# Cross-attention and feed-forward kernel: residual stream kept with features on partitions

## The reference

```python
x   # (8, 128, 512); ctx (8, 128, 512); 32 heads of 128
n = layernorm(x)                     # no weights
h = rmsnorm(n) * ln_weight
q, k, v = h @ w_q.T, ctx @ w_k.T, ctx @ w_v.T          # (8, 128, 32 x 128)
s = where(mask, q k^T + position_bias, -inf)           # per batch and head
x = x + n + (softmax(s), masked) v @ w_out.T           # x + (n + attention)
n = layernorm(x)
W = NF4_CODE[w_codes] * absmax (blocks of 64)          # 512 x 512
x = x + n @ W.T + 2.0 * n @ W_a @ W_b
return x
```

## Time and profile before

| what | value |
|---|---|
| median of 3 runs | 832.5 us (832.13 to 833.02) |
| profiled execution, its own time | 831.71 us |
| span from first to last instruction | 829.9 us |
| busy: PE, DVE, ACT, Pool | 824.1, 447.5, 445.6, 535.3 us |
| instructions | 15761 |
| DMA | 64.46 MB, 78 GB/s on the mean |

### The profile page before, as it was taken

How to read it: one execution, slowest core, us unless ns; L and a number is a source line. 1 busy time by engine, 2 the same in 40 slices (tenths; PEclk the granted TensorE clock), 3 DMA queues, 4 the chain that set the end, 5 groups by cost and what they waited for, 6 DMA issues and landing times.

```text
span 829.9 us, 15761 instructions
## 1 busy us (share of the span) xinstructions
PE 824.1 (99%) x4702; PEld 720.3 (87%) x4702; DVE 447.5 (54%) x754; ACT 445.6 (54%) x1297; POOL 535.3 (65%) x556
## 2 busy tenths in 40 slices
PE   9999999999999999999999999999999999999998
PEld 6888888988899888988889888998889888898886
DVE  5785655355634656245553556346562455636683
ACT  5766474464726555364644647355553646447632
POOL 0576778467875778756785578757787567855440
PEclk9999999999999999999999999999999999999999
DMA  8212332122211323113221222113230232311102
GB/s 326 90 42 90 107 94 68 54 92 66 93 36 58 98 68 97 26 69 98 79 89 54 92 66 92 38 55 97 69 96 24 71 98 68 104 41 51 46 13 89
DMA packets 50357, 64.46 MB, mean 78 GB/s; under 512 B 10752, under 2 KB 36480, under 8 KB 49312
## 3 DMA queue, kind: packets, MB, share of 16 engines
q1 hardware_dynamic: 50336, 64.20, 24.9%
HBM read 44.24 MB, written 4.19 MB: 58 GB/s over the span
## 4 chain that ended last, share of the span: by engine, by line
PE 94%; DVE 2%; ACT 2%; SPq 1%; DMA 0%; issue 0%; POOL 0%; POOLq 0%; ACTq 0%
PE w_ps L1184 44%; PE o_ps L1184 35%; PE s_ps L1220 6%; PE s_ps L1226 6%; SPq L342 1%; ACT p_blocks L652 1%; DVE stats L901 1%; DVE resid L1017 1%; PE s_ps L1184 1%; ACT p_blocks L603 1%; PE s_ps L1250 0%; PE o_ps L1250 0%; PE w_ps L1286 0%; PE w_ps L1241 0%; PE w_ps L1247 0%; DMA pT<-p_blocks 0%
## 5 line engine op out<-in xcount | busy, mean ns | idle before, releaser
L531 POOL TENSOR_SCALAR picked<-codes 128x256 f32<-128x256 int32 x112 | 124.3, 1110 | 19.2 <-POOL level L534 15.6
L496 POOL TENSOR_TENSOR p<-pos_raw,mask_add 128x1024 f32<-128x1024 f32 x32 | 69.6, 2175 | 103.1 <-ACT p_blocks L652 102.8
L652 ACT ACTIVATE p_blocks<-p,neg_max 128x128 f32<-128x128 f32 x248 | 96.1, 389 | 48.4 <-DVE neg_max L994 44.0
L534 POOL TENSOR_TENSOR level<-level,picked 128x256 f32<-128x256 f32 x112 | 90.6, 809 | 20.9 <-POOL picked L531 20.9
L468 POOL TENSOR_TENSOR ring_lo<-k_raw,ring_hi 128x256 fp32r<-128x256 f32 x105 | 76.5, 740 | 30.2 <-ACT ring_hi L603 27.3
L603 ACT ACTIVATE ring_hi<-k_raw 128x256 fp32r<-128x256 f32 x105 | 38.8, 414 | 101.0 <-POOL k_raw L458 101.0
L1017 DVE TENSOR_TENSOR resid<-o_ps,resid 128x512 f32<-128x512 f32 x102 | 68.7, 686 | 44.7 <-PE o_ps L1184 44.5
L1184 PE MATMUL w_ps<-ctx_hi,ring_hi 128*128 128x512 f32 x210 | 84.7, 403 | 0.0
L1184 PE MATMUL w_ps<-ctx_hi,ring_lo 128*128 128x512 f32 x210 | 82.1, 391 | 0.0
L1184 PE MATMUL w_ps<-ctx_lo,ring_hi 128*128 128x512 f32 x210 | 81.7, 389 | 0.0
L603 ACT ACTIVATE p_blocks<-p_blocks,row_scale 128x128 f32<-128x128 f32 x248 | 77.2, 391 | 1.1 <-DVE row_scale L1001 1.1
(11 more groups left out here) (229 smaller groups left out, 2289.8 us busy)
## 6 DMA issues: line engine op xcount, KB each, us to landing
pT<-p_blocks SPq DMA_DIRECT2D x480, 32.0 KB, 1.8
k_raw<-k_dram SPq DMA_DIRECT2D x16, 512.0 KB, 3.5
wv_raw<-wv_dram SPq DMA_DIRECT2D x8, 1024.0 KB, 4.8
q_raw<-q_dram SPq DMA_DIRECT2D x32, 256.0 KB, 3.7
wo_raw<-wo_dram SPq DMA_DIRECT2D x32, 256.0 KB, 4.0
resid<-x_dram SPq DMA_DIRECT2D x2, 1024.0 KB, 12.6
pos_raw<-pos_dram SPq DMA_DIRECT2D x32, 64.0 KB, 3.8
out_dram<-resid SPq DMA_DIRECT2D x8, 256.0 KB, 2.0
```

The lines of the kernel that those rows point to most:

```text
L496: pool.tensor_tensor(p[:, :, :], pos, mask_add[:, :, :], ALU.add).then_inc(bias_done, 1)
L531: then(pool.tensor_scalar((level if code == 0 else picked)[:, :], codes[:, :], float(code), NF4[code], match, ALU.mult))
L534: then(pool.tensor_tensor(level[:, :], level[:, :], picked[:, :], ALU.add))
L652: e = act.activation(out(b), p[:, b, :].rearrange("p (k c) -> p k c", c=Q), ACT.Exp, bias=neg_max[:, b:b + 1], accum_out=prob_sum[:, b:b + 1])
```

## The change

The residual stream is kept with features on partitions: `resid` is [128 features, 4 slices, 1024 tokens].

- Start: x is loaded as before to the same memory for statistics and staging, and then a second copy of x, transposed on the host (`xt_d`), is loaded over it. It is multiplied by 1 + rstd, which is now a value per column: the 1024 scales go through DRAM and come back as a row on all partitions (`scale_row`, in `wo_raw`). The shift by the mean is left out of the stream. `residual(c)`: four operations of 128x1024. The loads of the first output weights wait for them.
- Loop: `output(t)` has w_out stationary and the attention moving; t runs over four slices of features for the first half of the tokens and then for the second.
- Feed-forward weights: centred, that is, the mean over input features is subtracted from each column, so that the stream needs no centring before the product. Pool sums the slices (two adds in the last group ahead of the last decode, one after the last slice has come), TensorE multiplies the sum by a 128x128 matrix of 1/512 between the attends of the two halves, DVE subtracts it (`centre_ffn`) between the adds of the last pair, ACT makes the high and Pool the low parts. The splitting in the last group goes.
- Tail: the stream itself is split (`stream_high`, `stream_low`) and multiplied. The stream is turned back to tokens on partitions for the output (`turn_back`), ACT adds the shift of the first norm (`shift`, into `v`), DVE takes the statistics from that, Pool rstd, and one DVE operation makes product * rstd + v. `ffn_norm`, `ffn_transpose` and `xT_low` go.

The diff, cut to its core (declarations left out):

```diff
@@ -171,7 +174,12 @@
 ...
         x_stage = [wv_raw[:, i, :] for i in range(4)] + two_tiles(flat_blocks(pT[:, :, :, :])) + [v[:, b, :] for b in (4, 5)]
-        ffn_stage = [kT[:, i, f * D:(f + 1) * D] for i in range(2) for f in range(2)]
+        x_tokens = flat(resid[:, :, :]).rearrange("p (b d) -> p b d", b=B)
+
+        scale_row = flat(wo_raw[:, :, :])
+
+        ffn_sum = flat(k_raw[:, 0:2, :])
+        mean_of = absmax[:, 0:P]
@@ -368,15 +382,27 @@
 ...
+            sp.wait_ge(factors_done, 1)
+            sp.dma_start(scale_d.rearrange("(b l) -> l b", b=B), ln_scale[:, :],
+                         allow_slow_non_contiguous=True).then_inc(scale_moved, 16)
+
+            sp.wait_ge(staged, B)
+            for i in range(2):
+                sp.dma_start(resid[:, 2 * i:2 * i + 2, :], xt_d[:, 2 * i:2 * i + 2, :]).then_inc(xt_loaded[i], 16)
+
+            sp.wait_ge(scale_moved, 16)
             sp.wait_ge(ctx_lo_done, 5)
-            load_wo(0, 0)
-            load_wo(1, 1)
+            sp.dma_start(scale_row, scale_d.partition_broadcast(P)).then_inc(scale_moved, 16)
 ...
+
+            sp.wait_ge(hidden_done, C)
+            load_wo(0, 0)
+            load_wo(1, 1)
@@ -548,6 +574,13 @@
 ...
                             split_k(m, p_at, key_slot(j, p_at))
+                    if last and j == 2:
+
+                        passed(ffn_loaded, 16)
+                        passed(k_lo_done, PRODUCTS * PAIRS)
+                        pool.tensor_tensor(ffn_sum, wv_raw[:, 0, :], wv_raw[:, 1, :], ALU.add).then_inc(ffn_sums, 1)
+                        passed(ffn_sums, 1)
+                        pool.tensor_tensor(ffn_sum, ffn_sum, wv_raw[:, 2, :], ALU.add).then_inc(ffn_sums, 1)
@@ -589,13 +622,18 @@
 ...
+            pool.memset(mean_of, 1.0 / D).then_inc(mean_of_done, 1)
+            pool.wait_ge(last_ffn_loaded, 16)
+            pool.wait_ge(ffn_sums, 2)
+            pool.tensor_tensor(ffn_sum, ffn_sum, wv_raw[:, C - 1, :], ALU.add).then_inc(ffn_sums, 1)
+            for c in range(C):
+                pool.wait_ge(ffn_hi_done, c + 1)
+                lo(ffn_weights(ctx_lo, c), wv_raw[:, c, :], ffn_weights(ctx_hi, c)).then_inc(ffn_lo_done, 1)
 ...
                 norm(pool.tensor_scalar(rms_a[:, one], mean_var[:, b, 1:2], EPS, None, ALU.add))
-                norm(pool.tensor_tensor(rstd[:, one], rms_a[:, one], minus_half[:, one], ALU.pow))
-                pool.tensor_scalar(ln_shift[:, one], mean_var[:, b, 0:1], rstd[:, one], -1.0,
-                                   ALU.mult, ALU.mult).then_inc(norm_done, 1)
+                pool.tensor_tensor(rstd[:, one], rms_a[:, one], minus_half[:, one], ALU.pow).then_inc(norm_done, 1)
@@ -678,6 +716,7 @@
 ...
             def split_ffn(c):
+                act.wait_ge(ffn_centred, c + 1)
@@ -798,12 +837,6 @@
 ...
                     split_wo(i, 2 * g + j // 2 + 1, wo_hi)
-                if last:
-
-                    act.wait_ge(ffn_loaded, 16)
-                    act.wait_ge(keys_done, PRODUCTS * m + 2)
-                    for c in range(C - 1):
-                        split_ffn(c)
@@ -868,26 +901,33 @@
 ...
-            act.wait_ge(last_ffn_loaded, 16)
-            split_ffn(C - 1)
-
-            def ffn_norm(b):
-                act.wait_ge(norm_done, 2 + b + 1)
-                if b >= 4:
-                    act.wait_ge(ffn_turned, b - 4 + 1)
-                act.activation(ffn_stage[b % 4], resid[:, b, :], ACT.Identity, bias=ln_shift[:, b:b + 1],
-                               scale=rstd[:, b:b + 1]).then_inc(ffn_staged, 1)
-
-            ffn_norm(0)
-            ffn_norm(1)
-            for b in range(B):
-                if b in range(2, B - 1):
-                    ffn_norm(b + 1)
-                act.wait_ge(ffn_turned, b + 1)
-                copy(xn_hi[:, :, b * L:(b + 1) * L],
-                     w_ps[b % 2][:, :].rearrange("p (c t) -> p c t", c=C)).then_inc(xT_hi_done, 1)
-                if b == 1:
-                    ffn_norm(2)
+
+            act.wait_ge(keys_done, PRODUCTS * PAIRS)
+            for c in range(C):
+                split_ffn(c)
+
+            def stream_high(b):
+
+                act.wait_ge(out_added, B * (PAIRS - 1) + HB * (b // HB + 1))
+                at = slice(b * L, (b + 1) * L)
+                copy(xn_hi[:, :, at], resid[:, :, at]).then_inc(xT_hi_done, 1)
+
+            def shift(b):
+
+                act.wait_ge(returned, b + 1)
+                act.activation(v[:, b, :], w_ps[b % 2][:, :], ACT.Identity, bias=ln_shift[:, b:b + 1]).then_inc(shifted, 1)
+
+            act.wait_ge(queries_done, 2 * H)
+            act.wait_ge(attn_done, 2 * H)
+            stream_high(0)
+            shift(0)
+            for b in range(1, HB + 1):
+                stream_high(b)
+            for b in range(1, B):
+                shift(b)
+                if b + HB < B:
+                    stream_high(b + HB)
@@ -933,16 +965,17 @@
 ...
                 dve.wait_ge(power_done, 3)
-                x_norm(dve.tensor_scalar(ln_scale[:, :], rstd[:, :], 1.0, None, ALU.add), False)
-                x_norm(dve.scalar_tensor_tensor(ln_shift[:, :], mean_var[:, :, 0], -1.0, rstd[:, :],
-                                                ALU.mult, ALU.mult))
-
-            def residual(b):
-
-                dve.wait_ge(staged, b + 1)
-                dve.tensor_scalar(resid[:, b, :], resid[:, b, :], ln_scale[:, b:b + 1], ln_shift[:, b:b + 1],
-                                  ALU.mult, ALU.add).then_inc(hidden_done, 1)
+                dve.tensor_scalar(ln_scale[:, :], rstd[:, :], 1.0, None, ALU.add).then_inc(factors_done, 1)
+                dve.scalar_tensor_tensor(ln_shift[:, :], mean_var[:, :, 0], -1.0, rstd[:, :],
+                                         ALU.mult, ALU.mult).then_inc(factors_done, 1)
+
+            def residual(c):
+
+                dve.wait_ge(xt_loaded[c // 2], 16)
+                dve.wait_ge(scale_moved, 32)
+                dve.tensor_tensor(resid[:, c, :], resid[:, c, :], scale_row, ALU.mult).then_inc(hidden_done, 1)
@@ -1013,23 +1046,22 @@
 ...
-            def add(b, bank):
-                dve.tensor_tensor(resid[:, b, :], bank, resid[:, b, :], ALU.add).then_inc(out_added, 1)
-
-            def add_pair(o, b):
-
-                dve.wait_ge(out_done, B * o + b + 1)
-                if b == 0:
-                    dve.wait_ge(hidden_done, B)
-                add(b, tile_ps[b % 4])
+            def add_pair(o, t, bank):
+
+                dve.wait_ge(out_done, B * o + t + 1)
+                if t == 0:
+                    dve.wait_ge(hidden_done, C)
+                at = resid[:, t % C, half(t // C)]
+                dve.tensor_tensor(at, bank, at, ALU.add).then_inc(out_added, 1)
 ...
-            def split_ffn(c):
-                dve.wait_ge(ffn_hi_done, c + 1)
-                lo(ffn_weights(ctx_lo, c), wv_raw[:, c, :], ffn_weights(ctx_hi, c)).then_inc(ffn_lo_done, 1)
+            def centre_ffn(c):
+
+                dve.wait_ge(ffn_mean_done, 1)
+                dve.tensor_tensor(wv_raw[:, c, :], wv_raw[:, c, :], tile_ps[0], ALU.subtract).then_inc(ffn_centred, 1)
@@ -1061,14 +1093,15 @@
 ...
             dve.wait_ge(x_turned, C)
+            dve.wait_ge(ctx_sums, 1)
 ...
             xn_low(1)
-            for b in range(HB):
-                residual(b)
+            residual(0)
+            residual(1)
@@ -1076,10 +1109,9 @@
 ...
             scale_rows(0, 0)
-            residual(HB)
+            residual(2)
             scale_rows(0, 1)
-            for b in range(HB + 1, B):
-                residual(b)
+            residual(3)
@@ -1137,15 +1164,14 @@
 ...
-            def ffn_stats(b):
-                dve.wait_ge(out_added, B * (PAIRS - 1) + b + 1)
-                tile_stats(b, 2 * B + 2 * b)
-
-            def xT_low(b):
+            def stream_low(b):
 ...
                 at = slice(b * L, (b + 1) * L)
-                lo(xn_lo[:, :, at], w_ps[b % 2][:, :].rearrange("p (c t) -> p c t", c=C),
-                   xn_hi[:, :, at]).then_inc(xT_lo_done, 1)
+                lo(xn_lo[:, :, at], resid[:, :, at], xn_hi[:, :, at]).then_inc(xT_lo_done, 1)
+
+            def last_stats(b):
+                dve.wait_ge(shifted, b + 1)
+                tile_stats(b, 2 * B + 2 * b, v[:, b, :])
@@ -1153,25 +1179,28 @@
 ...
             for b in range(B):
-                add_pair(PAIRS - 2, b)
+                add_pair(PAIRS - 2, b, tile_ps[b % 4])
 ...
                 attention(2 * (H - 2) + 2 * hf + 1, 1, hf, s_flat(hf))
+            for t in range(B):
+                if t < C:
+                    centre_ffn(t)
+                add_pair(PAIRS - 1, t, tile_ps[(t + 1) % 4])
+                if t >= C:
+                    stream_low(t - C)
+            last_stats(0)
             for b in range(B):
-                add_pair(PAIRS - 1, b)
-                if b == 0:
-                    split_ffn(C - 1)
-                ffn_stats(b)
-                if b == FFN_TRANSPOSE_BEFORE - 1:
-                    xT_low(0)
-
```

(73 more changed lines are left out.)

48 lines of the change are left out of this document (22 added, 26 removed).

## The result

The changed kernel takes 837.6 us in the median of 4 runs (837.54 to 837.81), the kernel before on the same chip 832.3 us (4 runs). The ratio is 1.006, with a 95% interval of 1.0045 to 1.0075: slower by 5.3 us. The profiled execution took 837.54 us with a span of 835.7 us, 5.8 more than the span before. The forecast was 836.6 us, with 834.0 for the span. One run of the kernel before, beside the last three experiments, was slow at 2130.8 us; it is in no ratio and moves the median it stands in by less than 0.1 us.

A forecast was written before the change was run, and what follows sets the result against it. TensorE, busy 824.1 of 829.9 us, was taken as the bound. 1.85 + 0.95 + 1.70 - 0.38 = 4.1 us on the 832.5 median gave 836.6; own range 835.6 to 837.6 (0.68), 8-in-10 range 834.6 to 839.0.

The forecast's parts named there:

- Price 0: Loop: swapping the stationary and moving operands of the output products costs nothing; bound 13 ns a matmul either way.
- The rival that wo-stationary products are cheaper: Output products: 5.4 ns saved per matmul would pay the 4.1 us, so not slower; chance 0.06 in all.
- Wait A: Tail, mean matmul: TensorE waits for Pool's sum of the weight slices, after the last slice lands; 1.85 us.
- The mean matmul: Tail: one added fp32 matmul of 512 columns in TensorE's queue; 0.95 us, lower end 0.86.
- Wait B: Last pair: the fourth output needs the mean's bank and waits for all four centrings on DVE; 1.70 us.
- The wait of 0.38 us: Tail: TensorE's wait for the low part of the normalised tile goes away; -0.38 us.
- the end: After turn_back(7): last shift and statistics tie with the last product; price 0, upper bound 0.3 us.
- Price: 0, if the scale row is there in time: Start: the store, x loads, row broadcast and new multiplies cost nothing if all is done by residual(0), 44.66 us.
- rival (3): Start stalls: scale row late; from about 46 us each microsecond may cost one, due at 51 gives 841; chance 0.06.
- if DVE idles at residual(0): Start: a sign named in advance that, if seen in the profile after, would show the forecast wrong.
- bound of 0.5 us: Start, head 0: second row_scale may end some 0.45 us later if make_bias waits for residual(2); price 0, upper bound 0.5.
- The clock: Tail: the granted clock may fall after the two new gaps, 2 us more each, giving 838.6 to 840.6; chance 0.12.

The follow-up runs named there:

- the last three experiments: Four of 16 probability moves issued by ACT, on the kernel named e8 (832.2 us) and on the kernel before (831.9); and e8 unedited again (832.6).
- e3: Changed kernel with the mean matmul behind the attention of both halves instead of the first; 836.7 us, kernel before 832.6.
- e8: Changed kernel with scales turned on DVE before the store, mean matmul behind both halves, centrings first, mean as one fp32r matmul; 832.6 us, kernel before 832.0.
- e4: Changed kernel with all four centrings on DVE ahead of the first add of the last pair; 836.5 us, kernel before 832.6.
- e1: Changed kernel with scales stored as 128 rows of 32 bytes and the row read by DVE with a stride; 839.2 us, kernel before 832.6.
- e2: Changed kernel with the 4-byte store of the scales behind the two loads of x instead of ahead; 840.8 us, kernel before 832.6.
- e5: Changed kernel, unedited, measured again; 838.4 us, kernel before 832.0.
- e6: Changed kernel with scales turned on DVE and stored as 32 pieces of 128 bytes, no strided read; 837.2 us, kernel before 832.0.

## Why the prediction was right, and where it was not

**The loop.** Price 0 held: the shift of 1.34 us is the same at head 0 and at 754 us, and the output products have the mean of the earlier trace rows. The rival that wo-stationary products are cheaper is out by the same.

**Wait A.** 1.85 was forecast, 1.78 measured from start to start, and the mechanism is the one described: the landing of the last slice, then Pool's add. e3 shows it by covering it.

**The mean matmul.** 0.95 was forecast, 0.93 measured, and e8 shows that 0.57 of it is its number format.

**Wait B.** 1.70 was forecast, 1.75 measured. e4 takes it away by the order on DVE alone, and e3 leaves it in place.

**The wait of 0.38 us and the end.** The wait is gone, and the end costs 0.05. The two adds on Pool ahead of the last decode, 1.27 us each, cost nothing by themselves: the decode ended at 783.41 and SP stored at 783.76.

**The start: the step that failed.** "Price: 0, if the scale row is there in time" is where the forecast is short, with what stood against rival (3): that the two largest transfers took 12.6 us amid all others and SP had 15. The prediction named "if DVE idles at residual(0)" as a sign of being wrong, and DVE idled 3.44 us there. Two things were missed. SP did not have 15 us for the row: the row's buffer is free only at 40.15, which left it 4.5 us to 44.66. The kernel before showed this too, since there SP loads `wo_raw` behind the same wait, at 40.46. And the loads of x were not over by then: the 4-byte store is slower than its 4 KB suggest and holds what is issued behind it. The loads of x took 12.2 to 13.8 us in the four traces with the store in front, and 6.0 to 6.4 in those without; the row behind them took 6.8 to 8.4 us, and 3.6 in e1. It came at 47.84, and 1.34 us were lost. The rival's own rule, from about 46 us each microsecond may cost one, gives 1.9. It was the mechanism of the rival at a small size, on top of the forecast, and not in place of it. The 840.8 us of e2, where DVE started at 51.07, lie at the 841 that the rival gave for 51; that is nearer than the rule earns, since for the 5 us TensorE waited 3.9 in head 0 (2.52 and 1.36). The operation of `row_scale`, 1.99 us before, took 2.00 at 56.98, so its bound of 0.5 us was not needed; with the row late this says little of what it would do with the row in time.

**What was not foreseen** is the 0.49 us at the moves of the last group. The wait is 0.7 in e3 and 0.8 in e4 and e5, but 1.5 to 1.6 in e6 to e8. It also differs between two executions of one kernel, 1.18 in the changed kernel's first trace and 0.83 in e5, so one trace of each kernel does not show that the 0.49 comes from the change. It is short where SP's 16 issues take 10.7 to 10.8 us and long where they take 11.2 or more, and most of the difference is one long issue. Why that issue is long was not settled. It is in the kernel before as well (1270 ns), and none of the edits in e1 to e8 touched that code.

**The clock.** The rival had 0.12 and did not come about in the changed kernel: windows from 785 to 802 us all show 1.00, behind waits of 1.61 and 1.58. It was nearer than that looks, since e4 lost the clock behind a wait of 1.92 us and e1 behind one of 2.80, while e2 kept it through one of 2.5. What decides between them no run here shows. The Trainium skill (TensorE: Matmul & The Clock Gate, Part 1) has the low rate as the default and activity as what releases it; e4 and e1 agree in kind, with 0.50 behind their waits.

**The sum.** With the measured terms: 1.34 + 0.49 + 1.78 + 0.93 + 1.75 - 0.38 + 0.05 = 5.96, against 5.80 of span; the 0.16 between them have no place in the table. Without the first two, it is 4.1, as forecast. The number is right for a reason that is partly luck. The 837.6 us lie at the upper end of the forecast's own range, and e5 puts the same kernel at 838.4, outside it (the bounds named beside that range add up to 836.0 to 837.8). The wide range held both, but the room in it was for a fall of the clock, which did not come, and not for the start, which did.
